# Nine sparse token tiles for eight, and dense products 896 columns wide in two banks of 448

## What is computed

```python
sa, ca, ga, sb, cb, gb = (silu(c) @ wmod) in six parts
h = layernorm(x) * (1 + ca) + sa                 # x: 2048 x 128
x = x + ga * scan(h)                             # x_t = A_bar * x_{t-1} + B u_t, then C x + D u
h = layernorm(x) * (1 + cb) + sb
probs = sigmoid(h @ router_w.T + expert_bias)    # 2048 x 160
top_w, top_idx = top_k(probs, 8)
top_w = 2.5 * top_w / sum(top_w)
combine[t, top_idx[t]] = top_w[t]                # 2048 x 160, zero elsewhere
routed = sum over the experts e of
    (silu(h @ w_gate[e].T) * combine[:, e]) @ w_down[e].T     # 128 -> 64 -> 128
shared = silu(h @ w_gate_shared.T) @ w_down_shared.T
out = x + gb * (routed + shared)
```

## Time and profile before

| what | value |
|---|---|
| runs, device us | 420.68, 423.02, 423.54; median 423.02 |
| the profiled execution, device us | 420.65 |
| its span, first to last instruction | 418.7 |
| PE busy (matmuls) | 365.3 us, 87% |
| DVE busy | 340.8 us, 81% |
| ACT busy | 274.7 us, 66% |
| POOL busy | 228.3 us, 55% |
| HBM traffic over the span | 215 GB/s |

### The profile page before, as it was taken

The page is one execution under the profiler, slowest core; times in us unless marked ns, Lnnn a source line. Parts: engine busy times, 40 slices in busy tenths (PEclk is TensorE's granted clock), DMA queues, the critical chain, the costliest instruction groups (busy, mean ns, idle before and its releaser), DMA issues.

```text
span 418.7 us, 6422 instructions
## 1 busy us (share of the span) xinstructions
PE 365.3 (87%) x1875; PEld 294.1 (70%) x1875; DVE 340.8 (81%) x716; ACT 274.7 (66%) x387; POOL 228.3 (55%) x251
## 2 busy tenths in 40 slices
PE   5588677999999999999889979877799899999882
PEld 4277566788886877785688979876577677766661
DVE  4898969888878899985869968873379988998885
ACT  3227854678877777675835536553578998898781
POOL 3578505788887777714991000000418888888850
PEclk9569999999999999999989969999799999999998
DMA  7900057899997877794658999999598999989752
GB/s 214 351 2 2 9 167 202 229 278 283 274 270 224 233 225 215 218 249 156 205 156 231 343 356 315 359 329 291 144 219 197 213 213 218 207 207 208 193 141 76
DMA packets 66673, 90.23 MB, mean 215 GB/s; under 512 B 8274, under 2 KB 47378, under 8 KB 66644
## 3 DMA queue, kind: packets, MB, share of 16 engines
q1 hardware_dynamic: 43396, 72.05, 61.8%
q0 software_dynamic: 4096, 8.40, 8.2%
q10 hardware_dynamic: 19152, 9.44, 7.6%
HBM read 74.52 MB, written 15.34 MB: 215 GB/s over the span
## 4 chain that ended last, share of the span: by engine, by line
PE 33%; DVE 18%; DMA 17%; POOL 15%; issue 7%; ACT 6%; SPq 4%; ACTq 0%; DVEq 0%
PE ps L1554 12%; POOL arena L723 11%; DMA arena<-combine_scratch 7%; PE ps L1567 5%; DVE ps L1111 5%; PE ps L1700 5%; PE ps L1717 4%; POOL w_lo L685 4%; DVE g_lo L1117 4%; PE ps L1576 3%; DMA expert_rows<-work 3%; DMA x_sb<-x 2%; ACT ps L843 2%; SPq L534 2%; DVE arena L1075 1%
## 5 line engine op out<-in xcount | busy, mean ns | idle before, releaser
L723 POOL DMA_INDIRECT arena<-expert_rows,y_idx x64 | 63.7, 995 | 94.2 <-DMA expert_rows<-proj_sb 76.3
L843 ACT ACTIVATE ps<-ps 128x1024 f32<-128x1024 f32 x80 | 80.7, 1008 | 38.4 <-PE ps L1554 36.7
L1117 DVE TENSOR_TENSOR g_lo<-ps,g_hi 128x1024 fp32r<-128x1024 f32 x81 | 98.3, 1215 | 1.3 <-ACT g_hi L856 1.3
L856 ACT ACTIVATE g_hi<-ps 128x1024 fp32r<-128x1024 f32 x81 | 82.5, 1019 | 11.7 <-DVE ps L1111 11.7
L715 POOL DMA_INDIRECT dispatched<-xn,row_idx x64 | 61.9, 968 | 35.1 <-DVE row_idx L1174 18.1
L685 POOL TENSOR_TENSOR w_lo<-w_raw,w_hi 128x384 fp32r<-128x384 f32 x52 | 52.3, 1025 | 29.3 <-ACT w_hi L873 29.1
L1111 DVE TENSOR_TENSOR ps<-ps,arena 128x1024 f32<-128x1024 f32 x44 | 54.2, 1231 | 17.0 <-ACT ps L843 10.2
L1554 PE MATMUL ps<-h_hi,w_hi 128*128 128x512 f32 x162 | 54.4, 417 | 11.9 <-DVE g_lo L1117 7.3
L1567 PE MATMUL ps<-g_hi,w_hi 128*128 128x512 f32 x162 | 51.0, 396 | 3.7 <-ACT g_hi L856 3.7
L1576 PE MATMUL ps<-g_lo,w_hi 128*128 128x512 f32 x162 | 51.1, 397 | 1.2 <-DVE g_lo L1117 1.2
L1554 PE MATMUL ps<-h_lo,w_hi 128*128 128x512 f32 x162 | 51.8, 401 | 0.0
(11 more groups left out here) (221 smaller groups left out, 598.9 us busy)
## 6 DMA issues: line engine op xcount, KB each, us to landing
arena<-combine_scratch SPq DMA_DIRECT2D x88, 256.0 KB, 4.1
w_raw<-experts SPq DMA_DIRECT2D x35, 384.0 KB, 6.2
h2T<-combine_scratch SPq DMA_DIRECT2D x48, 256.0 KB, 5.1
xn<-combine_scratch SPq DMA_DIRECT2D x24, 256.0 KB
arena<-experts SPq DMA_DIRECT2D x36, 128.0 KB, 3.9
expert_rows<-work ACTq DMA_DIRECT2D x18, 256.0 KB, 5.2
h2T<-experts SPq DMA_DIRECT2D x20, 128.0 KB, 3.6
expert_rows<-wmod_sb ACTq DMA_DIRECT2D x9, 256.0 KB, 5.6
```

The source lines that it names most:

```text
L723: pool.indirect_dma_start(out=y_back(n, n + 1), out_offset=None, in_=y_rows[:, :], in_offset=bass.IndirectOffsetOnAxis(ap=y_idx[:, q, k:k ...
L843: act.activation(slot(z), slot(z), ACT.Silu).then_inc(silu_done, 1)
L856: act.activation(g_hi[:, k % RING, :].rearrange("p (b n) -> p b n", b=2), slot(z), ACT.Copy).then_inc(hi_ready, 1)
L1117: dve.tensor_tensor(g_lo[:, k % RING, :].rearrange("p (b n) -> p b n", b=2), slot(z), g_hi[:, k % RING, :].bitcast(F32).rearrange("p (b n) ...
```

## The change

Seven tiles are dense and nine are sparse. The dense products are 896 columns wide (`CHUNK`), in two banks of 448 each (`WIDE`) instead of 512; the number of pairs and of matmuls stays. The sparse tokens now make 72 sends and 72 fetches, 9,216 rows, 18 extra groups and 38 steps. Since eight tiles went in two groups of four and nine go in three groups of three, what was counted in fours on the sparse side is counted in threes (`PART_TILES`): the parts of POOL's row moves, the shared expert's groups, the sums (`add_back`). Fetches now signal in groups of six (`FETCHED`). The scalings on ACT begin one pair earlier and go seven with three pairs instead of two with one. POOL still issues six fetches behind each `w_lo` and five sends in the first half; the last run of fetches, behind the last `w_lo`, is 18 long instead of ten. Several buffers move (extra weight blocks, sorted rows, late combine rows), with the sorted-row ring nine deep instead of ten. Group 1 of the router (tiles 4 to 7) now has its last tile on the sparse side. The core of the diff:

```diff
-CHUNK = 2 * BANK
-GC = CHUNK // BANK
-DT = CHUNK // P
+DT = 7
+CHUNK = DT * P
+WIDE = CHUNK // 2
+GC = 2
...
+PART_TILES = 3
-SH_GROUPS = ST // BLK
+SH_GROUPS = ST // PART_TILES
-XIN, WOG, ZB, YST = 10, 6, 3, 4
+XIN, WOG, ZB, YST = 9, 6, 3, 4
+FETCHED = 2 * PART_TILES
-PARTS = ((0, 3), (3, 6), (6, 8))
-YTILES = 2
+PARTS = ((0, 3), (3, 6), (6, 9))
+YTILES = 3
-SEND_FIRST, SEND_MORE = 4, 5
+SEND_FIRST, SEND_MORE, FETCH_MORE = 4, 5, 6
...
+        def scaled_by(p):
+            return min(max(p - BACK_FROM + 1, 0) * 7 // 3, ST * TOPK)
...
-                if n in (26, 28, 30):
+                if n in (27, 29, 31):
                     sp.wait_ge(yg_done, SH_GROUPS + n + 1)
-                    pair = (26, 30, 28).index(n)
+                    pair = (27, 29, 31).index(n)
                     load_combine(first + pair, pair, True)
...
-                        ).then_inc(yk_loaded[n // GT], 16)
+                        ).then_inc(yk_loaded[n // FETCHED], 16)
...
                     if (i, s) >= (DRAIN_TURN + 1, 0):
-                        more = min(got + 6, ST * TOPK)
+                        more = min(got + FETCH_MORE, ST * TOPK)
                         fetch(got, more)
...
-                act.wait_ge(yk_loaded[n // GT], 16 * GT)
+                act.wait_ge(yk_loaded[n // FETCHED], 16 * FETCHED)
...
-                if p >= BACK_FROM:
-                    scale_back(2 * (p - BACK_FROM))
-                    scale_back(2 * (p - BACK_FROM) + 1)
-            for n in range(2 * (PAIRS - BODY * (DRAIN_TURN + 1) - BACK_FROM), ST * TOPK):
-                scale_back(n)
+                for n in range(scaled_by(p - 1), scaled_by(p)):
+                    scale_back(n)
...
-                    at = BODY * (i - DRAIN_TURN - 1) + k - BACK_FROM - 2
-                    if at >= 0 and at % 2 == 0:
+                    p = BODY * (i - DRAIN_TURN - 1) + k
+                    while PART_TILES * (back + 1) <= scaled_by(p - 2):
                         add_back(back)
                         back += 1
...
                 for n, (w, v) in enumerate(((hi, h2_hi), (hi, h2_lo), (lo, h2_hi))):
                     for b in range(2):
-                        last = pe.matmul(ps[:, 2 * z + b, :], w,
-                                         v[:, b * BANK:(b + 1) * BANK],
+                        last = pe.matmul(ps[:, 2 * z + b, 0:WIDE], w,
+                                         v[:, b * WIDE:(b + 1) * WIDE],
                                          start=(n == 0), stop=(n == 2))
```

More of the change, by code:

```diff
@@ L338, in adaln_layer @@
         y_stored = [sem(f"y_stored{s}") for s in range(YST)]
-        yk_loaded = [sem(f"yk_loaded{s}") for s in range(ST * TOPK // GT)]
+        yk_loaded = [sem(f"yk_loaded{s}") for s in range(ST * TOPK // FETCHED)]
         out_stored = sem("out_stored")
@@ L451, in x_dram, with out_dram @@
             return a[0, tok(g), :].rearrange("(q p) h -> p q h", p=P)
+        def out_dram(first, end):
+            return out[0, first * P:end * P, :].rearrange("(q p) h -> p q h", p=P)
         @block.sync
@@ L576, in _ @@
             turn(TURNS - 1, True, False, True)
-            for g in range(GC, GROUPS):
-                sp.wait_ge(sparse_ready, g - GC + 1)
-                sp.dma_start(x_dram(out, g), out_sb[:, tiles(g), :]).then_inc(out_stored, 16)
-            sp.wait_ge(out_ready, 1)
-            sp.dma_start(x_dram(out, 0), out_sb[:, tiles(0), :]).then_inc(out_stored, 16)
-            for half in range(2):
-                q = slice(half * GT // 2, (half + 1) * GT // 2)
-                sp.wait_ge(out_ready, GC + half)
-                sp.dma_start(x_dram(out, GC - 1)[:, q, :], out_sb[:, tiles(GC - 1), :][:, q, :]
+            for h in range(ST // PART_TILES):
+                first = DT + h * PART_TILES
+                sp.wait_ge(sparse_ready, h + 1)
+                sp.dma_start(out_dram(first, first + PART_TILES), out_sb[:, first:first + PART_TILES, :]
                              ).then_inc(out_stored, 16)
-            sp.wait_ge(out_stored, 16 * (GROUPS + 1))
+            for n, (first, end) in enumerate(((0, GT), (GT, GT + 2), (GT + 2, DT))):
+                sp.wait_ge(out_ready, n + 1)
+                sp.dma_start(out_dram(first, end), out_sb[:, first:end, :]).then_inc(out_stored, 16)
+            sp.wait_ge(out_stored, 16 * (ST // PART_TILES + 3))
         @block.gpsimd
@@ L827, in combine_weights @@
                     act.wait_ge(consts_set, 7)
-                for t in range(g * GT, (g + 1) * GT):
+                for t in dense_tiles(g):
                     last = act.activation(comb[:, t, SHARED:EC], picked_lo[:, t, :], ACT.Copy, scale=top_inv[:, t:t + 1])
@@ L1092, in top_eight @@
                 for t in range(GT):
-                    last = dve.match_replace(rest[:, t, :], top8[:, g * GT + t, :], p[:, t, :],
-                                             0.0 if g < GC else -1.0)
+                    dense = g * GT + t < DT
+                    last = dve.match_replace(rest[:, t, :] if dense else picked_hi[:, g * GT + t - DT, :],
+                                             top8[:, g * GT + t, :], p[:, t, :], 0.0 if dense else -1.0)
                 last.then_inc(rest_ready, 1)
@@ L1346, in _ @@
             dve.wait_ge(x_sent, 16 * ST * TOPK)
-            keep_shared(0)
-            keep_shared(1)
+            for n in range(SH_GROUPS):
+                keep_shared(n)
             for n in range(1, XT_GROUPS, 2):
@@ L1414, in _ @@
             add_ffn(1, 0, GT // 2)
-            add_ffn(1, GT // 2, GT)
-            for s in range(back, ST * TOPK // GT):
+            add_ffn(1, GT // 2, DT - GT)
+            for s in range(back, ST * TOPK // PART_TILES):
                 add_back(s)
@@ L1514, in turn_combine @@
                     pe.wait_ge(mod_1_ready, 1)
-                for q in range(GT):
-                    t = g * GT + q
+                for q, t in enumerate(dense_tiles(g)):
                     pe.transpose(ps[:, B_COMBT[g], q * P:(q + 1) * P], comb[:, t, 0:P], ident[:, :])
```

135 lines of the change are left out of this document (79 added, 56 removed).

## The result

The changed kernel takes 481.84 us (median of four runs, 479.62 to 485.37); beside it the kernel before took 422.14. The ratio is 1.1425, with a 95% interval of 1.137 to 1.148: slower by 60 us. The forecast was 486, range 460 to 503.

The account below looks back on a forecast made before the run. Bounds: PE in the first dense half, transfers in the sparse part, POOL's rounds in the second half. First fetch at 310.1, plus 170.0 and clock 3.3, is 483.4 us of span; with 1.95 around it 485.4, said as 486, range 460 to 503.

Parts of the forecast that it names:

- the first sparse step: Start of the sparse part: moves from 210.66 us by 8.6 us.
- the sparse part: First sparse step to POOL's first fetch: 38 steps for 36, 1.4 MB more at 337 GB/s, 4.1 us; bounds 0 and 5.
- the tail: After w_lo(26): 18 fetches, 23.0 us at 1.28 each, landing at 155.5; then 15.0 less 0.5 to the end.
- The ring: Second half: POOL's w_lo waits for ACT's w_hi, behind scalings awaiting fetches POOL just issued; 486 us, 466 to 500; chance 0.78.
- the five turns: Second half, groups 22 to 26: POOL waits through landing and ACT's catching up; 84.8 us where five rounds were 48.4.
- The landing after the last issue: Each turn of the second half: L between 1.5 and 5.2 us, taken as 2.4.
- The first half: POOL's sends end 9 us later, SP goes on 7.2 us late, pair 44 is 6.4 us late; ends 6 us later.
- What would show it: Signs: five w_lo waits of 5 to 10 us; gates of pairs 43 and 44 await late combine loads; first fetch near 310.
- the clock's 3.3 us: Second half: PE at half clock after idling lengthens one product for group 26 (1.8 us) and the last two pairs (1.5).
- rival B: Second half: the cold clock governs, lasting through turns and tail; 503 us; chance 0.05.
- Rival A: Second half: fetches land before ACT comes to them, so POOL runs unheld and the ring doesn't close; 445 us; chance 0.12.
- Rival C: Both halves run at PE's pace, if POOL's round is under 7.33 us; 399 us, faster; chance 0.03.

Follow-up runs that it names:

- r1: Changed kernel with two scalings a pair, as before the change, the ten left over behind the last pair: 442.56 us, ratio 1.047.
- r2: Changed kernel with eight fetches behind each low part instead of six, scalings as changed: 445.17 us, ratio 1.062.
- r3: Kernel before (eight tiles, 512 columns) with only the new pace of scalings and fetches signalling in sixes: 473.91 us, ratio 1.129.
- r4: Changed kernel where fetches 24 to 53 signal in threes instead of sixes, pace unchanged: 469.05 us, ratio 1.117.
- r6: Changed kernel with SP's wait for all sends and the first six sorted loads put after pair 44's combine load: 472.40 us, ratio 1.118.
- r8: Changed kernel with half the bytes of each extra weight block, in as many loads: 462.76 us (one run).
- r11: Changed kernel with two scalings a pair, combine loads first, nine fetches in POOL's first round, and low parts from group 2 on DVE: 407.09 us.

## Why the prediction was right

**The whole.** The span came out at 480.4 us, with 483.4 forecast, and that is closer than its terms: the first sparse step came 1.7 us earlier than forecast, the sparse part took 5.3 us more, the way from the first fetch to `w_lo` of group 26 took 1.5 less and the tail 5.1 less. The mechanism held; that the total lies within 1% is in part luck.

**The ring** is shown: undone by the order of scalings (r1) or by fetching further ahead (r2), made in the kernel before (r3), weakened by finer signals (r4). It is the pace that closes it, seven scalings with three pairs; the scalings begin no earlier, as the section on the change has it, but with two in pair 50 in both kernels. From the first fetch `w_lo` of group 26 ended after 128.6 us (130.1 forecast), the five turns took 83.1 (84.8). Turn by turn, from end to end of `w_lo`, they were 15.6, 15.0, 16.3, 16.2 and 20.0 us. The landing after the last issue was 3.4, 2.1 and three times 1.6 us (from the end of the issue to the blocked scaling: 429.62 to 431.24 in the turn shown), mean 2.0 where I took 2.4.

The issue-to-landing row answers to the earlier trace rows:

```profile
DMA to landing us min/median/max: 2.4/3.1/5.4
```

The DMA engines were busy for 0.30 to 0.46 of the turns (windows below), 0.92 of the same part before, and the median fell from 4.7 to 3.1 us. In the turns the last fetch landed 2.5 to 4.3 us after its issue began. The estimate of 2.15 us by the Trainium skill's "DMA: Bandwidth & Descriptors" (Anatomy of one DMA) lies below all five, but nearer to four of them than the median of before; the minimum of all fetches is 2.4.

**Two errors cancelled ahead of the turns.** `w_lo` of group 18 ended 13.8 us after the first fetch, not 16.0. But group 20 waited 3.24 us, where "for groups 19 to 21 the scalings reach only an older round" had 0.3: the older round landed only at 338.69 us (ACT had waited 5.31 us for it), and ACT then had three pairs to do before the high part of group 20, until 346.54 plus its own time, longer than POOL's next round. So group 21 ended at 45.5 us, with 45.3 forecast.

**The first half:** the last send began at 182.08 (182.3 forecast), SP went on at 184.31 (185.8), as the landing took 2.2 us instead of 3.5. The gates of pairs 43 and 44 waited 14.10 and 2.37 us for their combine loads, as "What would show it" had it. The first step came 6.9 us later than before (8.6). r6 confirms the place.

**The sparse part** is the term that looks most wrong: 9.4 us more in the two profiles, with 4.1 forecast and 5 as a bound. Over all runs with whole blocks, five of eight tiles take 86.8 to 90.9 us, mean 89.3, and eight of nine tiles 90.9 to 96.2, mean 93.5: 4.2 us. The one profile of before was the shortest of its kind, that of the change the longest. r8 bears out the bytes, in one run: 4.7 MB less took 15.8 us off that mean, where 337 GB/s gives 14.

**The tail:** from `w_lo` of group 26 to the end 38.1 us, with 43.2 forecast: the landing came 24.0 us later (25.4), the end 14.0 after that (14.5), and the clock's 3.3 us hardly show here; 1.8 of them were meant for the turn of group 26, where ACT waits 1.40 us for PE. The windows of three turns:

```profile
374.80:387.50 12.70, 6.97 (x29) 5.13 (x28) 7.40 (x10) 5.82 (x11) 5.78 (x7) 0.95 0.46 118
389.80:403.80 14.00, 6.43 (x25) 5.40 (x25) 5.26 (x7) 5.50 (x11) 5.72 (x7) 0.74 0.33 94
...
422.30:440.00 17.70, 8.25 (x31) 7.13 (x30) 7.38 (x10) 7.36 (x13) 5.67 (x6) 0.71 0.30 89
```

PE idles for about half of the turns (0.37 to 0.54 of each), and the mean granted clock of a turn falls to 0.71. In the last one PE had no work from 423.9 to 433.3 us; from 422 to 426 us the granted clock was 1.00, from 428 to 436 it was 0.50, the lower of its two levels (1.2 of 2.4 GHz), and from 438 to 440 again 1.00. That PE falls back to half clock after such a gap is the rule of the Trainium skill's "TensorE: Matmul & The Clock Gate" (Why this matters for your kernels), and these windows agree. But almost nothing on the path waits for PE there (the 1.40 us of ACT above), so rival B, the clock governing the half, did not come about. The clock is a consequence here.

**Rival A** (445) is what r1 and r2 made. **Rival C** (399) had as its condition that POOL's round falls under PE's. No run met it as such in the second half; in r11 POOL issues without a wait and no engine waits for it, and the time is 407.

## What to carry to other kernels

When one queue feeds another and waits for its product, read how far apart they stand in whole rounds: here a change of pace that looks harmless moved a wait from the round before to the round just issued, larger signals made that wait longer (alone, in r1, they closed no ring), and together they cost 40 us while every engine's busy share fell (PE from 87 to 76%, POOL from 55 to 50%). A narrower matmul pays only where PE's pace is the round's: compare each round's own length on every engine (7.33 against 8.2 and 9.4 to 9.7 us) before counting the saving. And of a term read from two single profiles, look at its spread over other runs before explaining it.
